# Running sums of the typed edge sweeps held in one PSUM bank and copied out by ScalarE

## The reference, cut to what matters

```python
q_dst = Q[dst]
kt = _typed_transform(K[src], W_E[l], edge_type)
scores = jnp.sum(q_dst * kt, axis=-1) / scale
scores = scores * mu[l].T[edge_type]
m = jax.ops.segment_max(scores, dst, num_segments=N)
e = jnp.exp(scores - m[dst])
s = jax.ops.segment_sum(e, dst, num_segments=N)
w = e / (s[dst] + 1e-10)
agg = jax.ops.segment_sum(V[src] * w[..., None], dst, num_segments=N)
```

## Time and profile before

| | us |
|---|---|
| median of 3 runs | 7317.35 (7316.95 to 7345.25) |
| the profiled execution | 7313.39, of which its span 7311.6 |
| DVE busy | 4841.4 (66%) |
| PE busy | 5467.1 (75%) |
| POOL busy | 3686.8 (50%) |
| ACT busy | 2775.2 (38%) |
| `L1286`, all seven sweeps, 1624 times | 654.2 busy |
| first and last `L1206` (typed sweeps, 3 x 232) | 3384.2 and 6129.4 |

### The profile page before, as it was taken

One profiled execution on the slowest core, in us unless ns is written; L12 is line 12 of the kernel. 1 busy time (PEld: TensorE's weight loads), 2 busy tenths in 40 slices (PEclk: granted clock), 3 DMA queues, 4 the chain that ended last, 5 costly groups with the idle time before them and its releaser, 6 DMA issues. The chain is left out here.

```text
span 7311.6 us, 115062 instructions
## 1 busy us (share of the span) xinstructions
PE 5467.1 (75%) x25450; PEld 4274.3 (58%) x25451; DVE 4841.4 (66%) x13284; ACT 2775.2 (38%) x9159; POOL 3686.8 (50%) x3856
## 2 busy tenths in 40 slices
PE   2788377769998488856777897777987777867775
PEld 1566366747776266645555685555775555734465
DVE  7666267747776566646999657999559997733313
ACT  0111166635666155523444234443334443300025
POOL 0577277726665177714666105665016663367730
PEclk9999989979999577777999998999999999966677
DMA  1000245546555155635777326776237775023330
GB/s 31 3 3 3 38 151 154 152 81 178 174 172 132 54 159 158 154 79 190 224 225 224 75 70 215 226 226 181 71 99 230 226 227 147 14 84 104 105 56 18
DMA packets 453631, 933.98 MB, mean 128 GB/s; under 512 B 109900, under 2 KB 207110, under 8 KB 453126
## 3 DMA queue, kind: packets, MB, share of 16 engines
q0 software_dynamic: 209536, 582.56, 30.2%
q1 hardware_dynamic: 239520, 346.64, 14.5%
q10 hardware_dynamic: 4326, 2.03, 0.1%
HBM read 789.17 MB, written 141.76 MB: 127 GB/s over the span
## 5 line engine op out<-in xcount | busy, mean ns | idle before, releaser
L1099 PE MATMUL bank<-arena,onehots 128*128 128x264 f32 (+3 forms) x6496 | 2002.7, 439 | 232.3 <-DMA arena<-tab_l,slot_src 120.3
L1055 PE MATMUL bank<-arena,spreads 128*128 x5568 | 1480.8, 375 | 599.9 <-DVE raw L1269 345.5
L1015 POOL DMA_INDIRECT arena<-tab_l,slot_typed x1392 | 1317.3, 946 | 719.7 <-issue 300.8
L1099 PEld LDWEIGHTS bank<-arena,onehots 128*128 128x128 f32 x6496 | 1306.9, 221 | 601.3 <-issue 212.0
L1055 PEld LDWEIGHTS bank<-arena,spreads 128*128 128x128 f32 x5568 | 1030.6, 210 | 980.3 <-issue 857.3
L1015 POOL DMA_INDIRECT arena<-tab_l,slot_src x928 | 884.7, 953 | 478.0 <-issue 259.3
L871 ACT ACTIVATE onehots<-iota_row,slot_loc 128x128 f32<-128x128 f32 x1856 | 641.1, 392 | 948.6 <-PE bank L1099 928.5
L1286 DVE TENSOR_TENSOR acc<-acc,bank 128x264 f32 (+3 forms) x1624 | 654.2, 403 | 504.9 <-PE bank L1099 495.1
L1189 DVE TENSOR_TENSOR arena<-arena,bank 128x512 f32<-128x512 f32 x928 | 630.2, 679 | 181.0 <-ACT stats L1137 75.8
L1015 POOL DMA_INDIRECT arena<-tab_l0b,slot_src x464 | 467.5, 1008 | 349.1 <-POOLq L1503 112.9
L1015 POOL DMA_INDIRECT arena<-tab_l0a,slot_src x464 | 453.8, 978 | 279.3 <-POOLq L1503 122.0
(11 more groups left out here) (376 smaller groups left out, 8078.9 us busy)
## 6 DMA issues: line engine op xcount, KB each, us to landing
spreads<-spread_dram SPq DMA_DIRECT2D x580, 256.0 KB
tab_l<-arena SPq DMA_DIRECT2D x150, 384.0 KB, 3.3
spread_dram<-spreads SPq DMA_DIRECT2D x116, 256.0 KB
onehot_dram<-onehots SPq DMA_DIRECT2D x58, 512.0 KB, 3.7
onehots<-onehot_dram SPq DMA_DIRECT2D x58, 512.0 KB, 4.1
arena<-tab_l,slot_typed POOLq DMA_INDIRECT x1392, 4.1
arena<-tab_l,slot_src POOLq DMA_INDIRECT x928, 2.8
arena<-tab_l0a,slot_src POOLq DMA_INDIRECT x464, 2.6
```

The source lines that it names most:

```text
L1015: pool.indirect_dma_start(out=rows_sb[:, a, t, half:half + width], out_offset=None, in_=table[:, :], in_offset=bass.IndirectOffsetOnAxis(a ...
L1055: mm = pe.matmul(z[x.k % 2][:, t, 0:cw], spreads[:, x.k, t * P:t * P + P], qtab[:, block_no[w], 0:cw], start=True, stop=not gatv2)
L1099: mm = pe.matmul(sums[x.k % 2], onehots[:, x.a, GT * x.k + t, :], rhs, start=t == 0, stop=t == GT - 1)
```

## The change

For the typed sweep alone (`held`), the sums of the current block stay in PSUM bank 4 (`running`) for the whole sweep. TensorE adds to what is there (`start=False`). After each group ScalarE copies the bank to `acc[:, block]` and then multiplies it in place by `goes_on`, a column that is one where the next group goes to the same block and zero where it goes to another; only then may TensorE add the next group. DVE's add-up is gone; its rescaling for a batch is done in the bank, one slot earlier, between ScalarE's scaling and TensorE's sum of the batch's first group. The block numbers are loaded by ScalarE and no more by DVE. `goes_on` is made once, by two DVE instructions.

```diff
+                    link(dve.memset(goes_on[:, :], 0.0))
+                    link(dve.tensor_tensor(goes_on[:, 1:GRP], block_f[:, 1:GRP], block_f[:, 0:GRP - 1], ALU.is_equal))
...
+            held = hgt
+            running = PS[4][:, 0:wc]
...
-                            if needed(x.g - 1):
+                            if held:
+                                if needed(x.g):
+                                    pe.wait_ge(S["added_up"].sem, S["added_up"].at(x.g))
+                                if x.k == 0:
+                                    pe.wait_ge(S["rescaled"].sem, S["rescaled"].at(x.batch + 1))
+                            elif needed(x.g - 1):
                                 pe.wait_ge(S["added_up"].sem, S["added_up"].at(x.g - 1))
...
+                                if held:
+                                    mm = pe.matmul(running, onehots[:, x.a, GT * x.k + t, :], rhs, start=False,
+                                                   stop=t == GT - 1, skip_group_check=True)
...
+                        x = Group(i, w, LAG["keep"])
+                        if x.there and held:
+
+                            act.wait_ge(S["summed"].sem, S["summed"].at(x.g + 1))
+                            op = act.activation(acc[:, block_no[w], 0:wc], running, ACT.Copy)
+                            if not (isinstance(i, int) and x.g == NB * BG - 1):
+                                op = act.activation(running, running, ACT.Copy, scale=goes_on[:, ds(x.g + 1, 1)])
+                            op.then_inc(S["added_up"].sem, 1)
...
+                    if held:
+                        dve.memset(running, 0.0)
...
-                        x = Group(i, w, LAG["keep"])
-                        if x.there:
+                        x = Group(i, w, LAG["add_up"] if held else LAG["keep"])
+                        if x.there and not (held and x.k > 0):
                             if needed(x.g):
                                 dve.wait_ge(S["added_up"].sem, S["added_up"].at(x.g))
-                            av = acc[:, block_no[x.k if gin else w], 0:wc]
+                            av = running if held else acc[:, block_no[x.k if gin else w], 0:wc]
...
+                        if x.there and not held:
                             dve.wait_ge(S["summed"].sem, S["summed"].at(x.g + 1))
                             dve.tensor_tensor(av, av, sums[x.k % 2], ALU.add).then_inc(S["added_up"].sem, 1)
```

More of the change, by code:

```diff
@@ L1098, in slot_fn @@
                                 rhs = rows_sb[:, x.a, GT * x.k + t, 0:wc] if gin else weighted[:, x.k % 2, t, 0:wc]
-                                mm = pe.matmul(sums[x.k % 2], onehots[:, x.a, GT * x.k + t, :], rhs,
-                                               start=t == 0, stop=t == GT - 1)
+                                if held:
+                                    mm = pe.matmul(running, onehots[:, x.a, GT * x.k + t, :], rhs, start=False,
+                                                   stop=t == GT - 1, skip_group_check=True)
+                                else:
+                                    mm = pe.matmul(sums[x.k % 2], onehots[:, x.a, GT * x.k + t, :], rhs,
+                                                   start=t == 0, stop=t == GT - 1)
                             mm.then_inc(S["summed"].sem, 1)
@@ L1106, in _ @@
                 def _(act):
+                    block_no = None
                     def slot_fn(i, w):
+                        nonlocal block_no
+                        if held and w == 0 and not (isinstance(i, int) and G16 * i < LAG["keep"]):
+                            block_no = next_blocks(mybir.EngineType.Activation, 0, G16 * i - LAG["keep"], G16)
+                        x = Group(i, w, LAG["keep"])
[5 more added lines that the diff above has]
+                            op.then_inc(S["added_up"].sem, 1)
                         x = Group(i, w, LAG["turn"])
@@ L1269, in slot_fn @@
                             dve.tensor_reduce(r, lane_split(pr, C), AX, ALU.add).then_inc(S["raw_made"].sem, 1)
-                        if w % (BG if gin else G16) == 0 and not (isinstance(i, int) and G16 * i + w < LAG["keep"]):
+                        if w % (BG if gin else G16) == 0 and not held and not (isinstance(i, int) and G16 * i + w < LAG["keep"]):
                             block_no = next_blocks(mybir.EngineType.DVE, 0, G16 * i + w - LAG["keep"], BG if gin else G16)
-                        x = Group(i, w, LAG["keep"])
-                        if x.there:
+                        x = Group(i, w, LAG["add_up"] if held else LAG["keep"])
+                        if x.there and not (held and x.k > 0):
                             if needed(x.g):
                                 dve.wait_ge(S["added_up"].sem, S["added_up"].at(x.g))
-                            av = acc[:, block_no[x.k if gin else w], 0:wc]
+                            av = running if held else acc[:, block_no[x.k if gin else w], 0:wc]
                             if x.k == 0 and not gin:
@@ L1283, in slot_fn @@
                                                   ALU.mult).then_inc(S["rescaled"].sem, 1)
-                                dve.wait_ge(S["rescaled"].sem, S["rescaled"].at(x.batch + 1))
+                                if not held:
+                                    dve.wait_ge(S["rescaled"].sem, S["rescaled"].at(x.batch + 1))
+                        if x.there and not held:
                             dve.wait_ge(S["summed"].sem, S["summed"].at(x.g + 1))
```

1 line of the change is left out of this document (added).

## The result

| | before | after |
|---|---|---|
| median, us | 7317.15 (7307.75 to 7345.25) | 7487.24 (7481.08 to 7516.61) |
| ratio | 1 | 1.0237, 95% 1.0203 to 1.027 |
| profiled execution, its span | 7313.39, 7311.6 | 7516.61, 7514.8 |
| one typed sweep, memset to dense sweep | 697 to 700 | 763 to 770 |
| of it slot 5 of the first batch to slot 5 of the last (28 batches) | 648 to 650 | 698 to 705 |

The changed kernel is 2.4% slower: 170 us in the medians, 203 between the two profiled executions (the changed kernel's, at 7516.61, is the slowest of its four). The 203 lie in the three typed sweeps: 161 in the 84 batches between the slots 5 (1.9 us each), 43 at the ends of the sweeps, 204 in all.

What follows compares the result with a forecast made beforehand. The prediction took DVE to carry a typed sweep. Terms of 14 (batches), 30 (sweep ends) and 75 us (clock), 119 in all, on the profiled 7313.39 gave 7432; the median's 4 us more made 7436, range 7288 to 7570.

Steps and rivals of the forecast that it cites:

- The saving: DVE's add-up leaves the typed sweeps: 0.33 us in each of eight slots per batch, 230 us if nothing else mattered.
- The pair: ScalarE's copy and in-place scaling after each sum: 0.38 and 0.47 us, ending 0.76 after the start.
- The chain: Each sum waits for ScalarE's work on the sum before: 2.09 us per group, leaving 0.04 us gain in ordinary slots.
- The detour in slot 6: ScalarE's copy and scaling go ahead of its one-hots and powers, delaying the batch's first weighing by 0.66 us.
- The rescaling: Now after DVE's slot 7 work, on TensorE's path: the first sum starts 2.2 us later, after 2.0 idle.
- The next batch only 0.36 later: Slot 3 0.70 us late, less 0.34, less 0.2 for block numbers: +0.16 us per batch, 14 us over 87.
- The clock: TensorE's clock falls after the new gap in two batches of three: 0.87 us per batch, 75 us.
- The end of a sweep: The last ten groups go from 1.2 us to 2.1 to 2.2 each: 10 us per sweep, 30 in all.
- the third rival: TensorE sinks to the lower clock for longer, in every batch and at sweep ends: 7530 to 7613 us; 20%.
- the gain comes through: ScalarE's copy and scaling take 0.47 us or less in all and the clock holds: 7260 us; 12%.
- The chain, but no second fall: Sums wait on ScalarE, but TensorE's clock does not fall a second time per batch: 7361 us; 20%.
- It does nothing: DVE's waits in the typed sweeps simply change name: 7317 us; 3%.

Runs made afterwards that it cites:

- b1_noadd: The kernel before with DVE's add-up left out of the typed sweeps; 0.994 of the kernel before, in a long set (kernel before at 8724 to 8807 us).
- after_beside: The changed kernel run again, unaltered, beside the kernel before; 7483.2 us against 7325.82, ratio 1.0221.
- a1_fill: The changed kernel plus three extra 256-column TensorE products ahead of each batch's first sum; 0.997 of the kernel before, in a long set.
- a5_early: The changed kernel with DVE's rescaling moved up in slot 7, between the product and the weighing; 7333.05 us against the kernel before's 7316.24, ratio 1.0023.
- a9_thin: a5_early plus three filler products in slot 5 and two ahead of each of a typed sweep's last 13 sums; 0.9919 of the kernel before, long set.
- a7_tail: a5_early plus six filler products ahead of each of a typed sweep's last 13 sums; 1.0032 of the kernel before, in a long set.

## Why the prediction was right, and where it was off

The forecast was 7436 us, the measurement 7487, inside the range, and the direction was right. Its steps, against the traces:

- **The saving**, 0.33 us in each of eight slots: DVE's work fell by it. DVE is at 157 of 200 us, near the 80% forecast, and b1_noadd has 0.36 for the add-up.
- **The pair**, 0.38 and 0.47, ending 0.76 after its start: 0.39 and 0.45, ending 0.74 after.
- **The chain**, 2.09 us: in columns 2 and 3 the sums stand 2.14 apart in median. Before, these columns held 2.72 and 2.93 in the mean. In the batch of the forecast TensorE waited there for DVE, for the reduction behind the rescaling and for the scores' layout:

```profile
4624.90 1.13 PE L1055 MATMUL bank<-arena,spreads 128*128 x4 [0.58 <-DVE raw L1269]
...
4627.56 0.33 PE L1032 MATMUL bank<-ident,arena 128*128 128x128 f32 x1 [0.65 <-DVE arena L1330]
```

After the change DVE has no add-ups and no rescaling in these slots, only the chain is left, and 1.3 us come back. The forecast had this in its times, 2.2 late at the first sum and 0.70 at the product of slot 3.
- **The detour in slot 6**, +0.66: from DVE's product of slot 5 to the first weighing 4.79 us before and 5.41 after in the mean, +0.62.
- **The rescaling**, first sum 2.2 later and a gap of 2.0: from DVE's product of slot 7 to the first sum 0.88 us before and 2.37 after, with the detour 2.11; column 7 says 2.25, and the gap is 2.09 in the batch shown. Right, and the largest step.
- **The next batch only 0.36 later**, and 0.16 net of DVE's load. This is the net of all steps but the clock, and the term that was most too small. Without the clock's 1.25 a batch is 0.71 longer (in after_beside 1.68 - 0.95 = 0.73). Part of it the forecast had not seen: TensorE's own load of 16 block numbers, once in two batches, which cost little before and now stands in line behind the first sum (the "issue" of 0.90). Column 0 in the batches with a load is 2.32 before and 2.93 in a1_fill, where the clock holds, in the others 2.16 and 2.14: 0.3 us per batch, 26 in all. Most of the clock's price falls in these batches too: against a1_fill columns 0 and 1 are 1.83 longer with a load and 0.71 without. No run takes the load away, so how much of the fall needs it stays open. The other 0.25 was not traced to one step.
- **The clock**, 0.87 per batch from a fall in two batches of three: 0.81 of the second sums ran at the lower level and the price was 1.25 per batch, 109 us over 87 batches instead of 75. The mechanism was right. In after_beside, near the median, the share is 0.63 and the price 0.95, 83 us: close to the two in three and the 75 that were forecast. A fall costs 1.5 us in both traces, where 1.3 was assumed.
- **The end of a sweep**, 30 us: 43. The clock fell to 0.50 there, as the third rival had it, which makes the chain 3.11 us and not 2.1 to 2.2.

So: forecast 1.03 us in a batch and 10 at the end of a sweep, measured 1.96 and 14 (in after_beside 1.68 in a batch). Forecast 119 us in all, measured 170 in the medians. The number fell inside the range because the range was wide; all three terms of its sum were too small, the one for the batch without the clock by the most (14 us against 62). Two of the signs named were wrong. TensorE hardly ever waits for ScalarE's scaling in mid-sweep (0.6 us in eight batches), as its product of the next slot stands between; and the idle ahead of a batch's first weighing is 1.6 us, not over 2; the forecast's own detour, 0.90 + 0.66, gives 1.56.

The Trainium skill (TensorE: Matmul & The Clock Gate, "A second HAM failure mode: psum-queue depth-cycling") says that small idles between groups of matmuls make the clock swing. By that rule the term of the clock is spent, and the trace agrees: 0.59 over the stretch behind the two gaps, 1.00 in a1_fill with the gap filled. But a1_fill kept 1.00 over idles of 0.79 and 0.88 us, so not every idle of this size brings a fall.

The rivals: "the gain comes through" fails not at the pair, which cost what was assumed, but at the rescaling's place, since a5_early has the same pair and ends within 0.3% of the kernel before. "The chain, but no second fall" is refuted by the shares in the table. "Sinks longer" was right at the end of a sweep alone. "It does nothing" is refuted by the ratio.

## What to carry to other kernels

When a change puts an accumulator behind a chain of engines, look first for the rare step on it, here one rescaling in eight groups, and put it where its engine comes by early. Moving this one instruction up was worth 154 us. Look also for rare instructions that hid behind other work, here the load of block numbers: they come to light where the chain has no slack. A wait on TensorE costs its own length and, if the clock falls behind it, more on top, here 0.95 to 1.25 us on 2.2 per batch. Useless products that just fit into the wait kept the clock up (a1_fill, a9_thin), and too many pushed the sums further apart than the low clock did (3.48 us against 3.11 in a7_tail).

## What the runs showed of the hardware

- ScalarE scales 264 columns in place in PSUM in 0.45 us and copies them from PSUM to SBUF in 0.39; back to back the scaling starts 0.29 after the copy.
- A 256-column product of 32-bit numbers is two matmuls, which at full clock start 0.22 us apart (a1_fill, a7_tail, a9_thin); that decided whether a filler fitted.
- With TensorE busy for 21 of 31 us in spells of 2.1 us and pauses of 1.0, the clock stayed at 0.50 to the end of the sweep; with the pauses filled it was 1.00 all through.
- The load of 16 block numbers holds TensorE's queue for 1.1 us (one line of code, all its instructions: shortest, median and longest in ns):

```profile
L899 PEldq TENSOR_LOAD <-block_of x90: 1101/1107/1286, 914.0 to 6286.8; - x90
```

- The same chip gave 7316 us for the kernel before in one set and 8729 in another. In the long sets the engines stop together about once in each batch. In a1_fill's trace TensorE, DVE and ScalarE all stand still for over 1 us 329 times, 1173 us in all, against 38 times and 216 us in the kernel before. What they wait for is not in the traces, and the stops do not account for all of the 1.4 ms; it stays open.
